# Exponentials in buffers of their own, a stage barrier taken out, statistics in parts and turned pieces spread anew, in a two-layer graph network

## The reference

```python
h = relu(layernorm(x))
x = x + relu(h @ W_S.T + b_S + segment_sum((h @ W_N.T + b_N)[dst] * exp(-w), src))
h = relu(layernorm(x))
q, k, v = h @ Wq + bq, h @ Wk + bk, h @ Wv + bv
logits = sum(q[dst] * k[src]) / sqrt(128)        # one per edge
alpha = softmax of logits over the edges with the same dst
x = x + elu(segment_sum(alpha * v[src], dst) + h @ Ws + bs)
```

## Time and profile before

| | |
|---|---|
| Runs of the kernel before | 821.2 us median of 3 (820.94 to 824.87) |
| The profiled execution's own time | 818.05 us |
| Its span in the profile | 816.2 us |
| TensorE busy | 737.1 us, 90% of the span |
| VectorE, ScalarE, GpSimd busy | 76%, 64%, 31% |
| Mean granted TensorE clock | 0.984 of 2.4 GHz |

### The profile page before, as it was taken

How to read it: one execution, slowest core, us unless ns; L and a number is a source line. 1 busy time by engine, 2 the same in 40 slices (tenths; PEclk the granted TensorE clock), 3 DMA queues, 4 the chain that set the end, 5 groups by cost and what they waited for, 6 DMA issues and landing times.

```text
span 816.2 us, 24230 instructions
## 1 busy us (share of the span) xinstructions
PE 737.1 (90%) x9625; PEld 721.6 (88%) x9625; DVE 618.0 (76%) x778; ACT 526.0 (64%) x1056; POOL 255.2 (31%) x206
## 2 busy tenths in 40 slices
PE   0178999999999999999999688699999999999996
PEld 0068999999999999999999567599999999999996
DVE  6778879889889989989984643777677677767771
ACT  4978757667766766766766234566676667666654
POOL 4763000000000000000000240376667667666766
PEclk9999999999999999999999789999999999999999
DMA  9822223113113113113113070404434433443300
GB/s 263 276 87 83 83 88 157 81 80 161 80 80 161 80 80 161 80 80 161 80 80 162 4 322 1 161 2 169 150 115 154 167 131 122 164 166 109 142 8 12
DMA packets 17667, 96.79 MB, mean 119 GB/s; under 512 B 2482, under 2 KB 8860, under 8 KB 11100
## 3 DMA queue, kind: packets, MB, share of 16 engines
q1 hardware_dynamic: 14572, 90.08, 29.0%
q0 software_dynamic: 3056, 6.17, 2.8%
HBM read 51.62 MB, written 44.63 MB: 118 GB/s over the span
## 4 chain that ended last, share of the span: by engine, by line
PE 84%; ACT 6%; DVE 5%; issue 2%; DMA 1%; POOLq 1%; POOL 0%; ACTq 0%; DVEq 0%
PE bank L1311 18%; PE bank L1154 17%; PE bank L1300 17%; PE bank L1171 9%; PE bank L1169 9%; PE bank L1133 8%; PE bank L1264 1%; PE bank L1259 1%; ACT kT L558 1%; ACT wst L615 1%; ACT gst L613 1%; PE bank L1119 1%; DVE junk L765 1%; ACT qT L547 1%; DMA samp_f<-in_samples 1%
## 5 line engine op out<-in xcount | busy, mean ns | idle before, releaser
L497 POOL TENSOR_TENSOR sm<-sm,mbc 128x768 f32<-128x768 f32 x100 | 174.4, 1776 | 119.6 <-ACT mbc L724 119.6
L1169 PE MATMUL bank<-oh_key,oh_lo 128*128 128x100 bf16 x1600 | 170.8, 208 | 8.0 <-ACT wst L615 6.9
L1171 PE MATMUL bank<-oh_key,oh_lo 128*128 128x50 bf16 x3200 | 171.1, 187 | 0.0
L1169 PEld LDWEIGHTS bank<-oh_key,oh_lo 128*128 128x128 bf16 x1600 | 155.7, 97 | 10.5 <-ACT wst L615 8.6
L1171 PEld LDWEIGHTS bank<-oh_key,oh_lo 128*128 128x128 bf16 x3200 | 164.0, 97 | 0.9
L1300 PE MATMUL bank<-qT,kT 128*128 (+1 forms) x1250 | 154.2, 277 | 8.1 <-ACT bank L676 8.1
L1300 PEld LDWEIGHTS bank<-qT,kT 128*128 128x128 f32 x1250 | 147.0, 193 | 9.6 <-ACT bank L676 8.6
L1311 PE MATMUL bank<-vals,sm 128*128 128x129 f32 x1250 | 154.8, 281 | 0.0
L1311 PEld LDWEIGHTS bank<-vals,sm 128*128 128x128 f32 x1250 | 150.9, 196 | 0.0
L939 DVE TENSOR_TENSOR oh_key<-oh_key,xt 128x1600 bf16<-128x1600 bf16 x150 | 141.9, 1001 | 0.0
L613 ACT ACTIVATE gst<-bank,tiny_col 128x400 f32<-128x400 f32 x200 | 122.2, 611 | 23.8 <-PE bank L1171 20.5
(11 more groups left out here) (123 smaller groups left out, 775.5 us busy)
## 6 DMA issues: line engine op xcount, KB each, us to landing
gt<-gst SPq DMA_DIRECT2D x25, 1600.0 KB, 5.5
gl_sb<-gt SPq DMA_DIRECT2D x25, 1600.0 KB, 6.7
records<-rec SPq DMA_DIRECT2D x1, 2015.0 KB, 7.5
out<-res SPq DMA_DIRECT2D x24, 64.0 KB, 1.5
src_i<-in_src SPq DMA_DIRECT2D x1, 403.0 KB, 6.2
w_in<-in_edge_weight SPq DMA_DIRECT2D x1, 403.0 KB, 6.6
dst_i<-in_dst SPq DMA_DIRECT2D x1, 403.0 KB, 7.1
dstn_i<-in_dst_next SPq DMA_DIRECT2D x1, 403.0 KB, 7.3
```

The costliest lines, as they stand in the source:

```text
L497: pool.tensor_tensor(part, part, top, ALU.subtract).then_inc(sub_done, 1)
L1169: T.matmul(cells, lo, oh_key[:, u, m, 0:2 * KEYS, i], start=True, stop=False, skip_group_check=True)
L1171: ins = T.matmul(cells[:, KEYS:2 * KEYS], lo, oh_key[:, u, m, (1 + w) * KEYS:(2 + w) * KEYS, i], start=False, stop=w == 2, skip_group_chec ...
```

## The change

It has four parts.

1. `TURNS` for odd tiles: piece 5 is turned and copied after group 7 with piece 6, no longer after group 5 with piece 4 (2, 2, 1, 2 pieces per slot, before 2, 2, 2, 1).
2. `end_stage` no longer waits. SyncE and GpSimd wait for `stage_end` by themselves: SyncE before it loads the count tables, GpSimd before its two fills of `vals` and `gl_sb`, which now stand behind all five `normalise_chunk`. TensorE's first `down` waits for a new semaphore, `sums_added`, which VectorE raises after a drain.
3. `statistics` is cut into `add_sums`, `moments` and `gather_moments`, put one by one between the tail sums; `inverse(0)`, the gathering of chunk 1, `inverse(1)` and the statistics of chunk 2 come behind the tail. ScalarE's `root(0)` and `root(1)` come behind its last piece, and `root(d)` from d = 2 waits for `xn_ready`, since the barrier no longer guards `ln_c`.
4. In stage 4 the mask writes to two buffers of `sm` in turn, and the exponential reads there with a step of 8 bytes and writes plainly to the other two (`weights`). The mask of tile t waits for the exponentials of tile t-2 of the same columns in place of `num_ready`; the exponential waits for the values of tile t-2.

```diff
-TURNS = (((0, 1), (2, 3), (4, 5), (6,)), ((0, 1), (2, 3), (4, 5), (6,)))
+TURNS = (((0, 1), (2, 3), (4, 5), (6,)), ((0, 1), (2, 3), (4,), (5, 6)))
...
-        def end_stage(eng, k):
+        def end_stage(eng):
             eng.drain().then_inc(stage_end, 1)
-            eng.wait_ge(stage_end, 5 * (k - 1))
...
         def twos(v, a, n):
-            return sm[:, v, a * P:(a + n) * P].rearrange("p (k d i) -> p k d i", d=P, i=2)
+            return sm[:, v % 2, a * P:(a + n) * P].rearrange("p (k d i) -> p k d i", d=P, i=2)
+
+        def weights(v, a, n):
+            return sm[:, 2 + v % 2, a * P:(a + n) * P]
...
-            end_stage(sp, 2)
+            end_stage(sp)
+            sp.wait_ge(stage_end, 5)
...
+            end_stage(pool)
...
             normalise_chunk(0)
             normalise_chunk(1)
-            end_stage(pool, 2)
+            for d in range(2, NC):
+                normalise_chunk(d)
+            pool.wait_ge(stage_end, 5)
             pool.memset(vals[:, :, D:D + 1], 1.0).then_inc(pad_ready, 1)
             pool.memset(gl_sb[:, :, NT * P:NTP * P], -FLOOR).then_inc(pad_ready, 1)
-            for d in range(2, NC):
-                normalise_chunk(d)
...
             def root(d):
+                if d >= 2:
+                    act.wait_ge(xn_ready, d - 1)
                 act.wait_ge(ln_step, d * 3 + 3)
...
                     act_piece(NT - 1, 0, j, LAST, used)
-                    if j >= NPC - 2:
-                        root(j - NPC + 2)
...
-            end_stage(act, 2)
+            end_stage(act)
+            root(0)
+            root(1)
...
                         act.wait_ge(sub_done, 2 * NSG + s * NSG + g + 1)
-                        part = sm[:, w, a * P:(a + n) * P]
-                        nc.scalar.activation(part, part, ACT.Exp).then_inc(exp_done, 1)
+                        act.wait_ge(num_ready, RING + s - 1)
+                        nc.scalar.activation(weights(w, a, n).rearrange("p (k i d) -> p k i d", d=P, i=2),
+                                             twos(w, a, n).rearrange("p k d i -> p k i d"), ACT.Exp).then_inc(exp_done, 1)
...
                     tail_sum(i)
-                    if i in (3, 5):
-                        first_chunks(i // 2 - 1, NPC + 2 + TAIL_FROM + i + 1)
-                first_chunks(2, NPC + 2 + TAIL_FROM + len(TAIL_SUMS))
+                    if i == 3:
+                        dve.wait_ge(l0_add, NPC + 2 + TAIL_FROM + i + 1)
+                        add_sums(0)
+                    if i == 4:
+                        moments(0)
+                    if i == 5:
+                        gather_moments(0)
+                    if i == 7:
+                        add_sums(1)
+                    if i == 9:
+                        moments(1)
...
-            end_stage(dve, 2)
+            end_stage(dve)
+            inverse(0)
+            gather_moments(1)
+            inverse(1)
+            dve.drain().then_inc(sums_added, 1)
+            statistics(2)
...
             def mask(t, v, g):
                 a, n = SG[g]
                 dve.wait_ge(s_ready, t * NSG + g + 1)
+                if not isinstance(t, int) or t >= 2:
+                    dve.wait_ge(exp_done, (t - 2) * NSG + g + 1)
...
                 if now:
                     dve.wait_ge(gl[v], turn * 16 + 16)
-                    dve.wait_ge(num_ready, t + 1)
...
-            end_stage(pe, 2)
+            end_stage(pe)
...
                 across(2, WK_, d, k_mm)
                 if d >= 1:
                     pe.wait_ge(proj_v, d * 2)
+                else:
+                    pe.wait_ge(sums_added, 1)
                 down(3, WV_, d, v_mm)
...
-                    weights = twos(v, h - h % 2, 2).rearrange("p k d i -> p (k d) i")[:, :, h % 2]
-                    ins = T.matmul(ps(4 + v % 2)[:, 0:D + 1], weights, vals[:, h, :], start=h == 0,
+                    ins = T.matmul(ps(4 + v % 2)[:, 0:D + 1], weights(v, h, 1), vals[:, h, :], start=h == 0,
                                    stop=h == NT - 1)
```

More of the change, by code:

```diff
@@ L279, in build_gnn @@
         fs_wl = [sem("fs_wl0"), sem("fs_wl1")]
+        sums_added = sem("sums_added")
         ln_step, xn_scaled, xn_ready, ln_std, ln_inv, ln_done, xn_turned, hc_ready = (
@@ L666, in _ @@
                 act_turn(NT - 1, 0)
-                root(0)
-                root(1)
-            end_stage(act, 2)
+            end_stage(act)
+            root(0)
+            root(1)
             def seed(t, v, turn, g):
@@ L864, in rows_in, with add_sums @@
                 return pair(i)[:, 0:CW].rearrange("p (t f) -> p t f", f=D)
-            def statistics(d):
+            def add_sums(d):
                 flat = xs[:, tiles(d), :].rearrange("p t f -> p (t f)")
@@ L870, in statistics, with moments @@
                                        op1=ALU.add).then_inc(ln_step, 1)
+            def moments(d):
                 dve.wait_ge(ln_step, d * 3 + 1)
@@ L874, in statistics, with gather_moments @@
                 ins.then_inc(ln_step, 1)
+            def gather_moments(d):
+                if d >= 1:
+                    dve.wait_ge(ln_done, d)
                 dve.wait_ge(ln_step, d * 3 + 2)
@@ L878, in statistics @@
                 ins.then_inc(ln_step, 1)
+            def statistics(d):
+                add_sums(d)
+                moments(d)
+                gather_moments(d)
             def inverse(d):
@@ L889, in inverse @@
                                        op1=ALU.mult).then_inc(ln_done, 1)
-            def first_chunks(k, adds):
-                if k == 0:
-                    dve.wait_ge(l0_add, adds)
-                    statistics(0)
-                if k == 1:
-                    inverse(0)
-                    dve.wait_ge(l0_add, adds)
-                    statistics(1)
-                if k == 2:
-                    inverse(1)
-                    dve.wait_ge(l0_add, adds)
-                    statistics(2)
             def tail_sum(i):
@@ L1004, in _ @@
                     add_sum(NT - 1, j)
-                for k in range(3):
-                    first_chunks(k, NPC + 2 + NPC * NT)
-            end_stage(dve, 2)
+                dve.wait_ge(l0_add, NPC + 2 + NPC * NT)
+                statistics(0)
+                add_sums(1)
+                moments(1)
+            end_stage(dve)
[4 more added lines that the diff above has]
+            statistics(2)
             V.tensor_scalar(bcol[:, 2:3], bcol[:, 0:1], -float(D) ** -0.5, None, ALU.mult).then_inc(s_qb, 1)
```

## The result

The changed kernel takes 813.39 us (median of four runs, 809.9 to 815.35), the kernel before on the same chip 821.36: a ratio of 0.9887 (95% interval 0.986 to 0.9914), 1.1% less. Run again on another chip, the ratio was 0.9863 (0.9833 to 0.9892). The forecast was 816.2 with a range of 808.5 to 820.0: the time lies in the range, the sign was right, but 5.0 us were forecast and 8.0 came (11.6 on the other chip). The surplus comes from a term that the prediction had priced at nothing: how the weights of the value matmuls lie in memory.

A forecast was written before the change was run, and what follows sets the result against it. The prediction took TensorE's work as the bound, with a hole at the handover from stage 2 to stage 3. The handover's 5.0 us, all other terms 0, took 821.2 to 816.2 us, range 808.5 to 820.0.

The forecast's parts named there:

- What bounds the kernel: Whole kernel: TensorE is busy for 90% of the span; the handover from stage 2 to stage 3 is a hole.
- The handover: From stage 2 to stage 3: without the barrier, TensorE turns chunk 1 at 468.5 instead of 473.5, gaining 5.0 us.
- What I had in time by 0.4 us: Stage 3: chunk 2's statistics and ScalarE's root would finish before its copy of chunk 0, ready at 467.1.
- The ±1 us for the clock: After the handover: TensorE's lower clock may cost up to 1 us, or the denser tail may save as much.
- Part 1, nothing: Stall of 0.54 us per pair of tiles, ahead of the even tile's group 0: VectorE releases it, so moving pieces gains 0.
- The weights' loads: Stage 4 value matmuls: loading weights plainly saves between 0 and 7.0 us; taken as 0 from transposes of `wst`.
- The rule that spoke for 7.0: Stage 4 value matmuls: the gap grows only with column number, plus a constant, so the sum would be 7.0 us better.
- The exponential's read: ScalarE in stage 4: reading with a step of 8 bytes costs between nothing and 84% more; taken as nothing.
- The slack of the second seed: Stage 4: ScalarE's second seed ends at 547.55, TensorE reads it at 547.81, so 0.26 us are free.
- The slower rival: Stage 4: each exponential grows by 0.71 us and delays the second seed, 25.5 us in all, giving 841.7; 4%.
- The first, strided loads: Stage 4 value matmuls: interleaved weights do cost, so TensorE saves 7.0 us besides, giving 809.2; 16%.
- the forecast's own case: Whole kernel: the handover gives 5.0 us and all else nothing, for 816.2, within 814.8 to 817.6; 47%.

## Why the prediction was right, and where it failed

- **What bounds the kernel.** Right: TensorE's own work in the steps, the handover's hole beside it.
- **The handover, 5.0 us.** Right in size: alone 4.3 to 5.0. By its own steps: `inverse(0)` was forecast at 462.1 and came at 461.26 (aligned): the last tail add ended at 461.12 (466.85 + 0.27, less 6.00) and not at 461.6, and the drain and the jump cost 0.14 us (to 467.26) and not 0.5. GpSimd's first chunk came at 464.3, not 465.7. What I had in time by 0.4 us was then late: the statistics of chunk 2 end at 472.65, with `add_sums` at 1.86 us where it took 0.83. It starts at 469.13, 0.07 us after GpSimd's second pass over chunk 0 (469.06), and ends inside the first pass over chunk 1, which takes 1.84 and not 1.26. ScalarE's root and its copy of chunk 0 wait behind it, and TensorE waits 1.98 for that copy. Chunk 1 was turned at 467.7 aligned where 468.5 was forecast. The ±1 us for the clock was nearly enough: of 5.82 us, 4.61 were left at the end of stage 3. Most of the 1.21 lies in chunk 0's first `down`, whose ten matmuls took 2.34 us at the lower clock and 1.28 before. That the parts add up to 5.0 is in some measure luck, since the earlier `inverse(0)` and the late statistics stand against each other.
- **Part 1, nothing.** Right, and for the reason given: VectorE ends the stall.
- **The weights' loads, taken as 0 "by the row".** This is the step that failed. The bounds were 0 and 7.0 us; the upper one was true (7.6 by the groups). The row that I took for the nearest, transposes of `wst`, was far by its operation and by its step: a matmul at 100 bytes takes twice a plain one, a transpose 3 ns more (109 and 112), and at the 8 bytes in question a transpose takes 11 ns more. And the trace held a figure that the choice left without a cause: 5.6 ns in each value matmul. The rule that spoke for 7.0, that the gap grows with the number of columns alone, is the formula for a single matmul in the Trainium skill, "TensorE: Matmul & The Clock Gate", section "Back-to-back issue gap". For the column it is borne out: 129 plain columns take 111.7 ns, 128 in the kernel 111.3. But the same section says that in a stream of weight loads and matmuls both set the spacing, and that is what the runs show: the weights' step alone takes it from 111.7 to 117.7 ns.
- **The exponential's read, taken as 0.** Too low, by 0.05 us alone and 0.09 in the kernel, and far from the 84% of the upper bound. The slack of the second seed was sized well: 2 x 0.09 of 0.26 us went there, the rest with the shorter step, and it was just used up. It cost 0.08 us a step (11.58 against 11.50), some 1.8 us in 22 steps. The slower rival, which needed 0.13 us per exponential, did not decide. The Trainium skill, "SBUF — State Buffer", section "Door 1: The DMA port swizzle", lets 8 bytes run at full rate: here 888 ns against 842, so nearly; but it also names four float32 as free, and 16 bytes took 1561.
- **Rivals.** The first, strided loads (809.2, given 16%), is what happened: 5.0 us for the handover and 6.1 for part 4. Its 12.0 us less the 1.8 that the seed took are 10.2, where 8.0 and 11.6 were measured as medians. It was ranked below the case that had no cause for the 5.6 ns. That the first measurement, 813.39, lies nearer to the forecast's 816.2 than to this rival's 809.2 is luck: two of its four runs were long ones at a granted clock of 0.983 (814.82 and 815.35), the other two took 809.9 and 811.96. It lies outside the 814.8 to 817.6 of the forecast's own case, and the range held because it had been drawn to take this rival in.

## What to carry to other kernels

A row prices an operation only if operation and step in memory are the same: what 8 bytes cost a matmul's weights could not be read from transposes at 100. Where two groups of equal work differ by a few ns each and the trace gives no cause, that remainder times the count is the forecast's first rival, not its last. And after a change that shortens a step, look at what had slack in it: a wait with 0.26 us left is gone when the work ahead of it on one side gives 0.14 us and two instructions ahead of it on the other grow by 0.09 each.

## What the runs showed of the hardware

- Float32 weights at 8 bytes cost 4.8 ns per matmul instruction of 128 columns and 6.0 of 129; at 16 or 100 bytes it took twice the time (233, 240 against 113 ns). Transposes at 8 bytes took 120 ns, at 100 bytes 112, plain 109.
- ScalarE's exponential of 768 float32: 842 ns plain, 888 at 8 bytes, read or written, 1561 at 16, 1578 at 32.
- The clock in a ramp with gaps of 1 to 2 us is a matter of the execution: 3.5 us between two executions of one kernel, and with 36 idle matmuls in each of two tiles four profiled ramps differed by 1.0.
- VectorE's two-input pass and GpSimd's slow each other where they overlap; in these traces the one that started later took longer. VectorE's `add_sums` took 1.86 us and not 0.83 where a pass of GpSimd already ran (469.13 against 469.06). Where it had started 0.16 or 0.17 us ahead of GpSimd's, it took 0.82 and GpSimd's pass 1.77 and not 1.26 (482.64 and 482.81 in the changed kernel).
